# One batch in four of the attention probabilities: block transposes on VectorE and a round trip through DRAM in place of TensorE transposes

## The chip, the core and the metric

The program runs on one core of a Trainium2 chip. The metric is the device time of one execution in microseconds (us). The engines of the core are TensorE (PE in the profile; its weight loads are PEld), VectorE (DVE), ScalarE (ACT), GpSimd (POOL) and SyncE (SP). They work side by side and wait for each other by semaphores only; here SP issues all the transfers (DMAs), in one fixed order.

## What is computed

The inputs are `x` of 128 batches x 32 rows x 1024 columns and a context of 128 x 257 x 256, all float32. Three residual blocks follow each other:

```python
x = x + xattn(layernorm(x), ctx, ctx)   # 32 heads, 8 key groups, head size 32, softmax over 257 keys
x = x + s4(layernorm(x))                # a causal convolution of length 1024 along the columns, plus a skip
x = x + moe(layernorm(x))               # rank-8 experts: top 16 of 64, 512 bottleneck columns
```

The change concerns the first block alone. There, for each batch and each of the 8 key groups, the 4 heads of the group x 32 rows give 128 rows of scores over 256 keys (the 257th key is handled apart), and the probabilities of these 128 rows must be turned, keys onto partitions, before TensorE can multiply them with the values.

## The kernel before

Four batches x 32 rows make one tile of 128 rows, so there are 32 tiles. The work of a tile is spread over three iterations: iteration `it` does the attention of tile `it` up to its second batch, ends the attention of tile `it-1` (batches 2 and 3) and does its convolution, and does the experts of tile `it-2`. The head (tiles 0 and 1, with the preparation of the weights) and the tail (tile 31 and what is left) are written out one call after the other. The order of the calls on each engine is written out by hand and fixed; an engine that meets a wait stands still with all that is behind it in its order.

The attention of a tile, batch `b` of four:

- `scores(it, b)` (PE, 24 matmuls, L573) writes 8 groups x 256 scores into four PSUM banks that are held once, so it waits until the maxima of the batch before are done.
- `maximum(it, n)` (DVE, L1398), n = 8b + g, adds the mask, writes the negated scores to `ms` and their minimum to `negmax`. `exp(it, n)` (ACT, L851) writes the probabilities into `pr[:, b % 2, g, :]` and their sums into `den`.
- `pair_chunk(it, m)` (PE, L561) turns two groups of `pr`, four 128x128 transposes into one of four PSUM banks (`ps_p`); `pair_copy(it, m)` (ACT, L783) copies the bank, 128x512, to `pts`. m runs from 0 to 15, four for each batch.
- `attend(it, hh)` (PE, 32 matmuls for two calls, L593), hh = 2b and 2b + 1, multiplies `pts` with the context `cx`; `output(it, b)` (ACT) copies the result out.
- `move_den(it, b)` (SP, L381) moves the sums with four small transfers; `normalisers(it)` (DVE, L1454) needs them of all four batches. GpSimd then makes the share of the last key and the residual, and `out_half`, `u_stats`, `row_norm` and `u_chunk` lead into the convolution.

All other transposes (`out_chunk`, `u_chunk`, `z_chunk`, `gated_chunk`) use the same helper at L561. `convolve` is L632, `experts` L647, `expand` L660. `q_turn` (DVE, L1405) already turns the queries, 128x512, in 32x32 blocks, after a trip through DRAM (`store_q`, `move_q`). Which bank a product uses is looked up in the table `BANKS`, and a product waits for the reader of what the bank held before. The tables of banks and the orders are all that a call's place depends on.

Of the kernel before, what the change touches and what calls it, by code (L numbers as in the profile page):

```python
# [27 lines left out]
P = 128  # L28
BPT = P // SEQ
TILES = BATCHES // BPT  # L30
HALVES = 2
# [4 lines left out]
PAIRS = STEPS // 2  # L36
# [31 lines left out]
    "pair": (1, 0, 0, 1, 0, 2, 0, 3, 1, 0, 0, 1, 0, 3, 1, 0,),  # L68
    "out": (0, 1,),
    "u": (3, 1,),  # L70
    "z": (0, 3,),
    "g": (1,),
    "y": (2, 1,),
    "f": (3, 2,),
    "b": (1, 2,),
    "o": (3, 2, 1, 1,),
    "keys": (3,),
    "router": (3,),
    "sums": (1,),
    "dft": (0,),  # L80
    "rows": (1,),
    "strip": (2, 3, 2,),
    "w": (0, 2, 0, 1, 2, 3, 2, 2, 3, 2, 1, 2, 3, 0, 1, 3,),
# [17 lines left out]
def at(tile, per, k):  # L101

    return tile * per + k

# [7 lines left out]
def build(nc, io):  # L112
    ctx = ExitStack()
    with ctx:
# [65 lines left out]
        turn_q = nc.dram_tensor("turn_q", [BPT, SEQ, DIM], F32, kind="Internal").ap()  # L180
        turn = nc.dram_tensor("turn", [BPT, SEQ, HEADS], F32, kind="Internal").ap()
# [23 lines left out]
        e_done = sem("e_done")  # L205
        pt_done = sem("pt_done")
# [108 lines left out]
        def _(sp):  # L315
# [126 lines left out]
            def iteration(it, odd):  # L442
                if on(it - 1):
                    load_context(it - 1, 2)
                turn_last(it)
                if on(it - 1):
                    load_residual(it - 1)
                if on(it - 3):
                    store(it - 3)
                if on(it - 1):  # L450
                    move_den(it - 1, 2)
                    move_den(it - 1, 3)
                if on(it + 1):
                    load_keys(it + 1, 0)
                load_context(it, 0)
                load_context(it, 3)
                load_context(it, 1)
                if on(it + 1):
                    load_last(it + 1)
                    load_keys(it + 1, 1)  # L460
                    store_q(it + 1)
                    load_keys(it + 1, 2)
                    move_q(it + 1)
                move_den(it, 1)
                move_den(it, 0)
                if on(it + 2):
                    load_x(it + 2)
                if on(it + 1):
                    load_keys(it + 1, 3)
                    store_last(it + 1)  # L470
            load_s4(); load_x(0); load_router(); load_wide(); load_context(0, 2); load_mask(); load_keys(0, 0)
            load_last(0); load_weight(0); load_keys(0, 1); store_q(0); clear_kernel(); load_weight(1); load_weight(2)
            move_q(0); load_x(1); load_keys(0, 2); load_weight(3); store_last(0); load_context(0, 0); turn_last(0)
            load_keys(0, 3); load_context(0, 3); load_last(1); load_keys(1, 0); store_q(1); load_weight(4)
            load_keys(1, 1); move_q(1); load_x(2); load_context(0, 1); move_den(0, 0); load_weight(5); load_keys(1, 2)
            load_weight(6); load_weight(7); store_last(1); load_keys(1, 3); turn_last(1); store_kernel()
            move_den(0, 1); load_strip(); move_den(0, 2); load_residual(0); move_den(0, 3); load_keys(2, 0)
            load_context(1, 0); load_context(1, 1); load_keys(2, 1); load_keys(2, 2); load_last(2); store_q(2)
            load_context(1, 3); move_den(1, 0); move_q(2); load_keys(2, 3); load_x(3); move_den(1, 1); store_last(2)
            for it in range(HEAD, TAIL):  # L480
                iteration(it, odd=it % 2)
            load_residual(30); load_context(31, 0); store(28); turn_last(31); load_context(30, 2); move_den(30, 2)
# [1225 lines left out]
```

## Time and profile before

| | |
|---|---|
| median of 3 runs | 1290.93 us (1287.35 to 1291.11) |
| the profiled execution | 1286.13 us, of which 1284.3 us are the span from the first to the last instruction |
| busy share of the span | PE 96%, ACT 87%, DVE 76%, POOL 64% |
| granted TensorE clock | 0.993 of full speed in the mean, 1.00 after the first stretch |
| DMA | 166.38 MB, mean 130 GB/s |
| one iteration in the steady part | 37.73 us |

The page of a profile gives the busy time of each engine, the chain of work that ended last (followed back from the last instruction, at each step to what released it), the costliest groups of instructions and the transfers. Further views group instructions by line and shape, list the waits, or show the instructions of a stretch in order of time. A matmul's duration includes its way through the array, and matmuls overlap, so the cost of a matmul is read from the distance between starts or from the chain, not from its mean duration.

### The profile page before, as it was taken

The page shows a single profiled execution, that of the slowest core. Times are in us where ns is not written, and L with a number is a line of the kernel's source. Part 1 is how long each engine was busy: PE and PEld are TensorE (multiplying, and loading weights), DVE is VectorE, ACT ScalarE, POOL GpSimd, SP SyncE. Part 2 cuts the span into 40 slices and gives each one's busy share as a digit, 9 for nine tenths or more (in the row PEclk, how much of TensorE's full clock was granted, in tenths as well). Part 3 has the DMA queues.
Part 4 walks back from the last instruction along what each step waited for, and adds up shares of the span by engine and source line. Part 5 has one row for each costly group of instructions (what it writes and reads, how often), then busy time and mean ns, then how long its engine had stood idle before and what let it go on. Part 6 is the DMA issues. An engine that isn't in the chain of part 4 may idle for free.

```text
span 1284.3 us, 41514 instructions
## 1 busy us (share of the span) xinstructions
PE 1238.2 (96%) x13676; PEld 1075.3 (84%) x13676; DVE 976.1 (76%) x3424; ACT 1121.2 (87%) x3337; POOL 827.1 (64%) x1259
## 2 busy tenths in 40 slices
PE   4679999999999999999999999999999999999997
PEld 3568888888888888888888888888888888888886
DVE  7877777877777777777877877778777777777753
ACT  6999999999899989898998989999998999899851
POOL 5477667677666667766767766676776666677420
PEclk9799999999999999999999999999999999999999
DMA  7543444444443444444344444444444434444210
GB/s 246 158 148 114 139 120 137 139 130 139 130 139 109 148 138 123 130 146 125 117 139 155 122 122 147 117 133 139 137 138 123 139 118 139 138 124 127 55 60 33
DMA packets 150103, 166.38 MB, mean 130 GB/s; under 512 B 58217, under 2 KB 116082, under 8 KB 149890
## 3 DMA queue, kind: packets, MB, share of 16 engines
q1 hardware_dynamic: 149890, 163.72, 42.7%
q8 instruction: 112, 1.84, 0.6%
q14 instruction: 101, 0.83, 0.2%
HBM read 128.50 MB, written 34.08 MB: 127 GB/s over the span
## 4 chain that ended last, share of the span: by engine, by line
PE 93%; ACT 2%; DVE 2%; DMA 1%; issue 1%; POOL 0%; SPq 0%; DVEq 0%; ACTq 0%; POOLq 0%
PE ps_p L561 27%; PE ps_p L647 17%; PE ps_p L632 17%; PE ps_p L660 14%; PE ps_p L593 10%; PE ps_s L573 9%; ACT pr L851 1%; DMA tmp<-in_wide 0%; ACT pts L783 0%; DMA qx<-turn_q 0%; DVE ms L1398 0%; DVE x L1254 0%; PE ps_p L519 0%; DMA turn_q<-xq 0%; ACT xq L865 0%
## 5 line engine op out<-in xcount | busy, mean ns | idle before, releaser
L851 ACT ACTIVATE pr<-ms,negmax 128x256 f32<-128x256 f32 x1024 | 513.8, 505 | 1.4 <-DVE negmax L1398 1.3
L1398 DVE CUSTOM_DVE_ANT_0 ms<-ps_s,neg_mask,last 128x256 f32<-128x256 f32 x1024 | 455.2, 473 | 55.4 <-PE ps_s L573 55.1
L783 ACT ACTIVATE pts<-ps_p 128x512 f32<-128x512 f32 x512 | 296.4, 593 | 51.4 <-PE ps_p L561 47.5
L561 PE MATMUL ps_p<-ident,pr 128*128 128x128 f32 x2048 | 305.2, 277 | 9.6 <-ACT pr L851 3.5
L561 PEld LDWEIGHTS ps_p<-ident,pr 128*128 128x128 f32 x2048 | 239.2, 141 | 46.1 <-issue 13.7
L851 ACT ACTIVATION_READ_ACCUMULATOR pr<-ms,negmax 128x1 f32 x1024 | 200.4, 196 | 0.0
L1072 POOL TENSOR_TENSOR kt<-kr,kt 128x512 fp32r<-128x512 f32 x128 | 165.6, 1293 | 29.5 <-ACT kt L783 29.5
L647 PE MATMUL ps_p<-wa_hi,ut_hi 128*128 128x288 f32 x512 | 177.6, 347 | 1.4 <-DVE ut_lo L1214 1.4
L647 PE MATMUL ps_p<-wa_lo,ut_hi 128*128 128x288 f32 x512 | 151.2, 295 | 0.0
L647 PE MATMUL ps_p<-wa_hi,ut_lo 128*128 128x288 f32 x512 | 150.6, 294 | 0.0
L1114 POOL TENSOR_TENSOR lastp<-lastp 128x256 f32<-128x256 f32 (+4 forms) x320 | 129.8, 405 | 22.6
L593 PE MATMUL ps_p<-pts,cx 128*32 128x128 f32 x4096 | 138.4, 276 | 3.5 <-DVE wb_lo L1226 2.6
L632 PE MATMUL ps_p<-strip_hi,ut_hi 128*128 128x512 f32 (+2 forms) x384 | 138.2, 360 | 0.4 <-DVE tmp L1482 0.4
L1095 POOL TENSOR_TENSOR qs<-qr,qs 128x512 fp32r<-128x512 f32 x64 | 82.9, 1295 | 80.7 <-ACT qs L783 80.7
L632 PE MATMUL ps_p<-strip_hi,ut_lo 128*128 128x512 f32 (+2 forms) x384 | 133.4, 347 | 0.0
L632 PE MATMUL ps_p<-strip_lo,ut_hi 128*128 128x512 f32 (+2 forms) x384 | 133.4, 347 | 0.0
L573 PE MATMUL ps_s<-kt,qs 32*128 32x256 f32 x3072 | 128.0, 298 | 0.0
L783 ACT ACTIVATE ut_hi<-ps_p 128x512 fp32r<-128x512 f32 x128 | 76.2, 596 | 57.3 <-PE ps_p L561 57.3
L593 PEld LDWEIGHTS ps_p<-pts,cx 128*32 128x32 f32 x4096 | 104.1, 109 | 24.7 <-issue 18.3
L573 PEld LDWEIGHTS ps_s<-kt,qs 32*128 32x128 f32 x3072 | 101.6, 187 | 21.9 <-issue 21.8
L660 PE MATMUL ps_p<-wb_hi,zt_hi 128*128 128x512 f32 x256 | 110.9, 433 | 3.0 <-DVE zt_lo L1214 3.0
L1152 POOL TENSOR_TENSOR x<-x,tmp 128x512 f32<-128x512 f32 x64 | 81.0, 1291 | 45.7 <-DVE x L1464 45.7
(139 smaller groups left out, 2562.5 us busy)
## 6 DMA issues: line engine op xcount, KB each, us to landing
cx<-in_ctx SPq DMA_DIRECT2D x128, 256.0 KB, 3.1
kr<-in_keys SPq DMA_DIRECT2D x128, 256.0 KB, 3.7
xq<-in_x SPq DMA_DIRECT2D x32, 512.0 KB, 4.0
turn_q<-xq SPq DMA_DIRECT2D x32, 512.0 KB, 3.7
qx<-turn_q SPq DMA_DIRECT2D x128, 128.0 KB, 2.9
xr<-in_x SPq DMA_DIRECT2D x32, 512.0 KB, 4.3
out_x<-tmp SPq DMA_DIRECT2D x32, 512.0 KB, 5.1
dn<-den SPq DMA_DIRECT2D x512, 2.0 KB, 1.8
```

Source lines behind the costliest of these rows:

```text
L561: mm = pe.transpose(into[:, j * P:(j + 1) * P], source, ident[:, :])
L573: mm = pe.matmul(ps_s[:, quad, h * SW:(h + 1) * SW], qs[rs, it % 2, q_part, b, h, :, :].rearrange("p r s -> p (r s)"), kt[rs, b, k_part, h ...
L593: mm = pe.matmul(product("o", b, it)[HEAD_DIM * q:HEAD_DIM * (q + 1), h * P:(h + 1) * P], cx[:, b, j, g * HEAD_DIM:(g + 1) * HEAD_DIM], pt ...
L632: mm = pe.matmul(product("y", k, tile)[:, o0:512], u[:, c, :], s[:, s0:s0 + w], start=(c == 0 and j == 0), stop=(c == 4 * k + 3 and j == 2 ...
L647: mm = pe.matmul(product("f", k, tile)[:, 0:ZB], u[:, c, :], w[:, c, k * ZB:(k + 1) * ZB], start=(c == 0 and j == 0), stop=(c == FC - 1 an ...
L660: mm = pe.matmul(product("b", k, tile)[:, :], u[:, c, :], w[:, c, k * 512:(k + 1) * 512], start=(c == 0 and j == 0), stop=(c == BC - 1 and ...
L783: return act.activation(out, in_, ACT.Copy, scale=scale)
L851: act.activation(pr[:, b % 2, g, :], ms[:, n % MS, :], ACT.Exp, bias=negmax[:, n % MS:n % MS + 1], scale=-1.0, accum_out=den[:, b, g:g + 1 ...
L1072: pool.tensor_tensor(kt[:, b, 1, :, :], kr[:, at(tile, BPT, b) % KRS, :, :], kt[:, b, 0, :, :].bitcast(F32), ALU.subtract).then_inc(kl_don ...
L1095: pool.tensor_tensor(qs[:, tile % 2, 1, :, h, :, :], qr[:, :, :, :], qs[:, tile % 2, 0, :, h, :, :].bitcast(F32), ALU.subtract).then_inc(q ...
L1114: pool.tensor_tensor(near, near, far, ALU.add).then_inc(ls_done, 1)
L1398: dve.tensor_tensor_reduce(ms[:, n % MS, :], ps_s[:, g % GPH, g // GPH * SW:(g // GPH + 1) * SW], neg_mask[:, 0:SW], 1.0, last[:, it % 2, ...
```

## The change

For batch 2 of each tile (`TURNED = (2,)`) the four `pair_chunk` and the four `pair_copy` are gone. Instead:

1. `exp` of that batch writes its 256 probabilities in runs of 32 to strided places, so that each half of `pr` (four groups, 1024 columns) is laid out in 32x32 blocks by key block.
2. `p_turn(it, 0, h)` (DVE), for the halves h = 0 and 1, transposes 128x1024 in place, block by block.
3. `store_p(it, 0, h)` (SP) writes the half, 512 KB, to the DRAM tensor `turn_p`; `load_p(it, 0)` waits for both stores, and reads the whole back with four transfers of 256 KB, each onto 32 partitions of `pts`.
4. `attend(it, 4)` and `attend(it, 5)` wait for the load, and read `pts` through a strided view as their moving operand.

The table of banks and the orders on all engines are new. What matters of the order on SP: `load_p(it-1, 0)` stands before `move_den` of batches 2 and 3, and `store_p(it-1, 0, 0)` stands behind the store of the output, which waits for `third_residual`. `exp` now waits for the reader of its own half of `pr` (two batches back) and not for all of the batch before.

```diff
-PAIRS = STEPS // 2
+TURNED = (2,)
...
+            def store_p(it, k, h):
+                sp.wait_ge(p_turned[k][h], at(it, 1, 1))
+                if at(it, 64, 0) > 0:
+                    sp.wait_ge(p_loaded[k], at(it, 64, 0))
+                sp.dma_start(turn_p[k, :, :, h, :],
+                             pr[:, TURNED[k] % 2, GPH * h:GPH * (h + 1), :]).then_inc(p_stored[k][h], 16)
+
+            def load_p(it, k):
+                b = TURNED[k]
+                for h in range(HALVES):
+                    sp.wait_ge(p_stored[k][h], at(it, 16, 16))
+                if at(it, 2 * BPT, 2 * b - 2) > 0:
+                    sp.wait_ge(pv_done, at(it, 2 * BPT, 2 * b - 2))
+                own = pts[:, b % 2 * GPH:(b % 2 + 1) * GPH, :]
+                for i in range(GPH):
+                    sp.dma_start(own[SEQ * i:SEQ * (i + 1), :, :],
+                                 turn_p[k, :, i, :, :].rearrange("(r t) h c -> t r (h c)", r=REP)).then_inc(p_loaded[k], 16)
...
             def attend(it, hh):
                 b, h = hh // 2, hh % 2
-                pe.wait_ge(pc_done, at(it, PAIRS, 2 * hh + 2))
+                if b in TURNED:
+                    pe.wait_ge(p_loaded[TURNED.index(b)], at(it, 64, 64))
+                else:
+                    pe.wait_ge(pc_done, at(it, PAIRS, paired(2 * hh + 2)))
+                turned = pts[:, b % 2 * GPH:(b % 2 + 1) * GPH, :].rearrange("p r (h j q s) -> p h j q r s", h=HALVES, j=TBLK, q=GPH)
...
+                                       turned[:, h, j, q, :, :] if b in TURNED else
                                        pts[:, (2 * hh + q // 2) % PTS, (2 * (q % 2) + j) * P:(2 * (q % 2) + j + 1) * P],
...
-                act.activation(pr[:, b % 2, g, :], ms[:, n % MS, :], ACT.Exp,
+                out, masked = pr[:, b % 2, g, :], ms[:, n % MS, :]
+                if b in TURNED:
+                    out = pr[:, b % 2, g // GPH * GPH:(g // GPH + 1) * GPH, :].rearrange("p g c -> p (g c)").rearrange(
+                        "p (i j g t) -> p g j i t", i=GPH, j=TBLK, g=GPH)[:, g % GPH, :, :, :]
+                    masked = masked.rearrange("p (j i t) -> p j i t", j=TBLK, i=GPH)
+                act.activation(out, masked, ACT.Exp,
...
+            def p_turn(it, k, h):
+                b = TURNED[k]
+                dve.wait_ge(e_done, at(it, STEPS, GROUPS * b + GPH * (h + 1)))
+                half = pr[:, b % 2, GPH * h:GPH * (h + 1), :].rearrange("p g c -> p (g c)")
+                dve.transpose(half, half).then_inc(p_turned[k][h], 1)
```

The new orders, cut to the calls that the prediction speaks of. On PE, iteration `it` (steady part): `pair_chunk(it-1, 12)`; `scores(it, 0)`; `pair_chunk(it-1, 13)`, `14`; `experts(it-2, 1)` whole, 24 matmuls; `pair_chunk(it-1, 15)`; `pair_chunk(it, 0)`; `attend(it-1, 4)`, `5`; `pair_chunk(it, 1)`; `scores(it, 1)`; `attend(it-1, 6)`, `7`; `pair_chunk(it, 2)`, `3`, both `out_chunk` and `experts(it-2, 0)` in three parts; `scores(it, 2)`; `pair_chunk(it, 4)`; `gated_chunk`; `attend(it, 0)`, `1`; `pair_chunk(it, 5)`, `6`; `expand` 18 matmuls; `scores(it, 3)`; `pair_chunk(it, 7)`; both `u_chunk`; `expand` 6 matmuls; `convolve` whole; `z_chunk`; `attend(it, 2)`, `3`; `z_chunk`.

On DVE: ..., `maximum(it, 23)`, `third_residual(it-2, 0)`, `p_turn(it, 0, 0)`, `maximum(it, 24)`, `q_turn`, `u_low(0)`, `maximum(it, 25)`, `26`, `u_low(1)`, `maximum(it, 27)`, `p_turn(it, 0, 1)`, `third_residual(it-2, 1)`, `maximum(it, 28)`, ... On ACT: ..., `exp(it, 20)`, `row_norm`, `pair_copy(it, 6)`, `u_high(0)`, `exp(it, 21)`, `u_high(1)`, `k_high(it+1, 1)`, `exp(it, 22)`, `exp(it, 23)`, ... On SP: `store(it-3)`, `store_p(it-1, 0, 0)`, `store_p(it-1, 0, 1)`, `load_residual(it-1)`, `load_context(it-1, 2)`, `turn_last(it)`, `load_p(it-1, 0)`, `move_den(it-1, 2)`, `move_den(it-1, 3)`, ...

## Rows read from the trace of the kernel before

**Rows 1.** The page's busy us, share of the span and instructions, by engine.

```profile
PE 1238.2 (96%) x13676; PEld 1075.3 (84%) x13676; DVE 976.1 (76%) x3424; ACT 1121.2 (87%) x3337; POOL 827.1 (64%) x1259
```

**Rows 2.** The page's chain that ended last, by engine and by line.

```profile
PE 93%; ACT 2%; DVE 2%; DMA 1%; issue 1%; POOL 0%; SPq 0%; DVEq 0%; ACTq 0%; POOLq 0%
PE ps_p L561 27%; PE ps_p L647 17%; PE ps_p L632 17%; PE ps_p L660 14%; PE ps_p L593 10%; PE ps_s L573 9%; ACT pr L851 1%; DMA tmp<-in_wide 0%; ACT pts L783 0%; DMA qx<-turn_q 0%; DVE ms L1398 0%; DVE x L1254 0%; PE ps_p L519 0%; DMA turn_q<-xq 0%; ACT xq L865 0%
```

**Rows 3.** One steady period: busy us by engine, clock, DMA share, GB/s.

```profile
586.00:623.73 37.73, 37.73 (x425) 32.90 (x425) 28.83 (x105) 34.27 (x105) 25.75 (x40) 1.00 0.45 138
```

**Rows 4.** The chain, start us and us: the same piece 26 periods apart.

```profile
171.00 4.00 PE ps_p L632 x21
...
1151.89 4.00 PE ps_p L632 x21
```

**Rows 5.** Pieces of the chain within one period: start us, us, what.

```profile
590.43 1.01 PE ps_p L593 x32
...
592.03 0.91 PE ps_s L573 x20
...
594.36 0.44 PE ps_p L561 x4
594.79 0.80 PE ps_p L647 x6
...
611.26 0.58 PE ps_p L561 x4
611.85 2.77 PE ps_p L660 x12
```

**Rows 6.** Groups by line and shape: the exponentials, the removed copies, the block transpose.

```profile
L851 ACT ACTIVATE pr<-ms,negmax 128x256 f32<-128x256 f32 x1024 | 513.8, 505 | 1.4 <-DVE negmax L1398 1.3
...
L783 ACT ACTIVATE pts<-ps_p 128x512 f32<-128x512 f32 x512 | 296.4, 593 | 51.4 <-PE ps_p L561 47.5
...
L1405 DVE STREAM_TRANSPOSE qr<-qx 128x512 f32<-128x512 f32 x64 | 44.9, 702 | 1.7 <-DMA qx<-turn_q 1.2 <-issue 0.3
```

**Rows 7.** Instructions in order of time, ACT and DVE: start us, us.

```profile
586.91 0.59 ACT L783 ACTIVATE pts<-ps_p 128x512 f32<-128x512 f32 x1
587.39 0.51 ACT L851 ACTIVATE pr<-ms,negmax 128x256 f32<-128x256 f32 x1
...
586.51 0.69 DVE L1405 STREAM_TRANSPOSE qr<-qx 128x512 f32<-128x512 f32 x1
587.13 0.44 DVE L1398 CUSTOM_DVE_ANT_0 ms<-ps_s,neg_mask,last 128x256 f32<-128x256 f32 x1
```

**Rows 8.** SP's issues in order of time: start us, us, number of transfers.

```profile
589.40 0.34 SPq L436 DMA_DIRECT2D xr<-in_x  x1
589.80 0.42 SPq L440 DMA_DIRECT2D out_x<-tmp  x1
591.71 5.92 SPq L381 DMA_DIRECT2D dn<-den  x8
...
611.71 2.21 SPq L402 DMA_DIRECT2D qx<-turn_q  x4
```

**Rows 9.** Transfers, KB and us to landing (589.4 to 595.2, then all); one microsecond's rate.

```profile
xr<-in_x SPq DMA_DIRECT2D x1, 512.0 KB, 4.3
out_x<-tmp SPq DMA_DIRECT2D x1, 512.0 KB, 5.2
...
cx<-in_ctx SPq DMA_DIRECT2D x128, 256.0 KB, 3.1
...
593.00:594.00 1.00, 1.00 (x10) 1.00 (x11) 1.00 (x4) 0.87 (x4) 0.00 (x0) 1.00 1.02 414
```

**Rows 10.** Landing times of the output's stores, then of the context's loads.

```profile
DMA to landing us min/median/max: 2.6/5.1/7.3
...
DMA to landing us min/median/max: 2.6/3.1/6.7
```

**Rows 11.** Waits over the whole span: us in total, times, longest us.

```profile
DVE dn L1454 <- DMA dn<-den: 33.6, 29, 2.0
```

More of the change, by code:

```diff
@@ L103, in at, with paired @@
     return tile * per + k
+def paired(m):
+    return sum(k // GPH not in TURNED for k in range(m))
+PAIRS = paired(STEPS // 2)
 def wait(eng, sem, value):
@@ L446, in iteration @@
                 if on(it - 1):
[L447 to L450, printed above, removed]
+                    load_p(it - 1, 0)
                     move_den(it - 1, 2)
@@ L472, in _ @@
[L472 to L476, printed above, removed]
@@ L485, in _ @@
+            store(30); store(31)
             sp.wait_ge(out_stored, 16 * TILES)
@@ L755, in _ @@
[L755 to L758 removed]
+            weight_chunk(0, 0); keys_transpose(); weight_chunk(0, 1); router_product(); weight_chunk(1, 0)
@@ L759, in _ @@
+            u_chunk(0, 1); pair_chunk(1, 7); convolve(0, 0, 0, 4); convolve(0, 1, 0, 2); convolve(0, 1, 2, 8)
+            z_chunk(0, 0, 0); attend(1, 3); z_chunk(0, 1, 0)
             for it in range(HEAD, TAIL):
                 iteration(it, odd=it % 2)
-            pair_chunk(30, 11); pair_chunk(30, 12); scores(31, 0); experts(29, 1, 0, 1); pair_chunk(30, 13)
-            pair_chunk(30, 14); experts(29, 1, 1, 2); pair_chunk(30, 15); experts(29, 1, 2, 5); attend(30, 4)
-            attend(30, 5); experts(29, 1, 5, 8); pair_chunk(31, 0); scores(31, 1); experts(29, 0, 0, 2)
@@ L764, in _ @@
-            pair_chunk(31, 1); attend(30, 6); attend(30, 7); experts(29, 0, 2, 3); pair_chunk(31, 2)
-            pair_chunk(31, 3); experts(29, 0, 3, 5); out_chunk(30, 0); experts(29, 0, 5, 6); out_chunk(30, 1)
-            experts(29, 0, 6, 8); pair_chunk(31, 4); scores(31, 2); gated_chunk(29); pair_chunk(31, 5); attend(31, 0)
-            attend(31, 1); pair_chunk(31, 6); expand(29, 0, 0, 3); pair_chunk(31, 7); expand(29, 0, 3, 4)
-            expand(29, 1, 0, 3); pair_chunk(31, 8); u_chunk(30, 0); expand(29, 1, 3, 4); u_chunk(30, 1)
@@ L769, in _ @@
[L769 to L773 removed]
+            scores(31, 0); pair_chunk(30, 12); pair_chunk(30, 13); pair_chunk(30, 14); experts(29, 1, 0, 1)
@@ new lines, in _ @@
+            pair_chunk(31, 6); expand(29, 0, 0, 3); expand(29, 0, 3, 4); expand(29, 1, 0, 3); pair_chunk(31, 7)
+            u_chunk(30, 0); expand(29, 1, 3, 4); scores(31, 3); u_chunk(30, 1); convolve(30, 0, 0, 4)
+            convolve(30, 1, 0, 1); convolve(30, 1, 1, 8); z_chunk(30, 0, 0); attend(31, 2); z_chunk(30, 1, 0)
+            pair_chunk(31, 12); attend(31, 3); pair_chunk(31, 13); pair_chunk(31, 14); experts(30, 1, 0, 2)
+            experts(30, 1, 2, 4); experts(30, 1, 4, 8); pair_chunk(31, 15); attend(31, 4); attend(31, 5)
```

527 lines of the change are left out of this document (264 added, 263 removed).

## The prediction

> **What bounds the kernel now.** I read the page's busy shares first: PE is busy for 96% of the span, ACT for 87%, DVE for 76% [rows 1]. A busy share alone doesn't say what sets the end, so the chain of waits came next: 93% of it is PE, and 27 of 100 parts of the span are the transposes of L561 alone, more than any other line [rows 2]. Then one period of the steady part: PE is busy for all of its 37.73 us, at full granted clock, while DVE has 8.9 us free, ACT 3.5 and the 16 DMA engines 55% [rows 3]. The same piece of the chain returns after 26 periods at a distance of 980.89 us, 37.73 each [rows 4]: no period differs from the next. So PE is the bound for the 29 iterations of the loop, some 1094 us, and time taken from PE is time taken from the kernel, as long as nothing it waits for comes later than now.
>
> **What a turned batch gives back on PE.** In the chain a `pair_chunk` between other matmuls costs 0.44 us, though the mean duration of its four transposes would suggest more; one that follows `attend` costs 0.58 us [rows 5]. The extra 0.14 goes with the change of shape and not with the chunk: the number of places where something follows `scores` or `attend` stays about the same in the new order. I take 0.44. Four chunks a tile, 32 tiles: 128 x 0.44 = 56.3 us. A period would be 37.73 - 1.76 = 35.97 us. The moving around of `experts`, `expand` and `convolve` changes no instruction; I cost it at nothing, and keep 0.2 us a period to both sides for it.
>
> **ACT.** Four copies a tile go; from the start of one to the start of what follows is 0.48 us [rows 7], so 1.92 us a period. ACT is then busy for 34.27 - 1.92 = 32.35 of 35.97 us, 90%. Nothing on the path, since ACT isn't on it now. The eight `exp` of batch 2 write in runs of 32 to strided places. No row shows such a write. Below nothing is excluded, as it is the same 256 elements; above I bound it by the copy's cost for 512 elements against the exp's for 256, 0.59 to 0.51 us [rows 6, 7], 0.1 us each, 0.8 a period, and PE's cover holds both. I take nothing.
>
> **DVE.** Two block transposes of 128x1024 a tile. The one of 128x512 lasts 0.70 us in the mean and the next instruction starts 0.62 us after it [rows 6, 7]. Twice the columns: at most 2 x 0.62 = 1.24 us, and not less than 0.62; I take 1.2, so 2.4 a period, and DVE is busy for 31.2 of 35.97 us, 87%. That it still fits is not that it is free: the second one stands ahead of `third_residual(it-2, 1)`, on which the output's store waits, and ahead of `maximum(it, 28)` to `31`, on which the next `scores` wait. Its cover is the time in which PE does `convolve`, 36 matmuls, of which 21 take 4.0 us [rows 4]; DVE has four maxima, two residuals and two splits there. With the cover gone it would cost its 1.2 us each period, 35 us in all.
>
> **DMA.** 1 MB out and 1 MB back a tile, 67 MB more on 166. The engines' share goes from 0.45 to about 0.45 x 233/166 x 37.73/35.97 = 0.66. They have carried 414 GB/s in one microsecond [rows 9], so the bytes fit. The latency is what counts, and so does SP, a single queue: six more issues a tile, about 0.42 to 0.55 us each [rows 8], 3 us of a period.
>
> **The new path.** What is late if something is late: `attend(it-1, 4)` now waits for the load, and behind it stand all of PE's calls. I follow the path from the end of `exp(it-1, 23)`:
>
> - `p_turn(.., 1)`: 1.2 us (above).
> - `third_residual`, before which SP doesn't get past the output's store: 0.6 us, as a DVE instruction of 512 columns [rows 7].
> - SP issues the output's store and `store_p` of half 0: 0.9 us until the second half's issue begins.
> - Landing of that one. Of two transfers of 512 KB issued 0.4 us apart the first landed after 4.3 us and the second after 5.2 [rows 8, 9]. A third adds another 0.9: 6.1 us.
> - `load_p`: four issues of 0.44 to 0.55 us; the last begins 1.3 to 1.7 us after the first, and a 256 KB load lands in 3.1 us [rows 8, 9]. 1 MB at 414 GB/s needs 2.5 us, so the rate doesn't add much. 5.0 us.
>
> Sum 13.8 us. This closes a loop, since `exp(it, 23)` can't come before PE has done what lies between `attend(it-1, 4)` and the second `u_chunk` of the same iteration (ACT reads it in `u_high(1)`, ahead of exps 22 and 23). That is, by rows 5: three pairs of `attend` 3.0, three `scores` 2.7, twelve chunks of transposes 5.3, 24 matmuls of `experts` at 0.133 = 3.2, 18 of `expand` at 0.231 = 4.2, six changes of shape 0.9: 19.3 us. Behind it on ACT two copies and two exps, 2.0 us, and 0.2 to hand over: 21.5 us. The loop is 21.5 + 13.8 = 35.3 us long against PE's 35.97. It closes, with 0.7 us to spare. Landing times scatter from 2.6 to 7.3 us [rows 10], so now and then it won't. The same queue feeds a second loop: `move_den` of batches 2 and 3 stands behind `load_p`. DVE already waits for these sums in 29 tiles, 1.2 us in the mean [rows 11], and they will come later by the four issues, 2.2 us, plus what SP waits ahead of `load_p`. The maxima of batch 1, for which `scores(it, 2)` waits, now stand behind `normalisers`. For both together I charge 0.25 us a period, 7.5 us in all.
>
> **Head and tail** hold 8 of the 128 chunks, counted above. PE isn't always the bound there, so up to 3 us of their share may not come; the new order may give as much. Nothing taken.
>
> **The sum.** 1286.1 (the profiled execution) - 56.3 + 7.5 = 1237.3 us. The median of the runs is 1290.93, 0.37% above the profiled execution; 1237.3 x 1.0037 = 1242 us is the forecast. What a measurement of this kernel can tell from no change is about 0.3%, 4 us.
>
> **Rivals.**
>
> 1. *The turned path is a little longer than the loop allows, and takes part of the gain.* The path has room for 35.97 - 21.5 = 14.5 us. At 15.4 us the period is 36.9, the gain 0.83 us a period, and the time 1290.9 - 0.83 x 32 = 1264 us. For it: three stores at once were never seen in this kernel, and the second was already 0.9 us later than the first. Against: the room of 0.7 us.
>
> 2. *No change: each load goes at half rate.* The four loads land on 32 partitions each. If such a load runs at half of 414 GB/s, 1 MB takes 5.1 us and not 2.5, the path is 13.8 + 2.5 = 16.3, the period 37.8 us, and all that PE gave back is spent in front of `attend(it-1, 4)`: 1293 us. Against: the queries' loads, also four onto 32 partitions, go out in 2.21 us [rows 8] and DVE hardly waits for them, 1.2 us in the whole span [rows 6]. The Trainium skill has this rule ("SBUF — State Buffer", section "Door 1: The DMA port swizzle"): partitions 0 to 31, and 0 to 63 too, are reached through 8 of 16 ports, at about half the rate. By the page alone, the time would be this rival's; no row here shows a large load onto 32 partitions, so it keeps a chance of its own.
>
> 3. *Slower: `attend(it-1, 4)` waits, every iteration, longer than the four chunks lasted.* One mechanism: the chain turn, store, load in front of PE. It decides from a path of 37.73 - 21.5 = 16.2 us on. At 17 us the period is 38.5, +0.8 us in 29 periods, about 1314 us; with the slowest landings of rows 10 in place of mine (7.3 for 6.1, 6.7 for 3.1) the path is 18.6 and the period 40.1, about 1360 us. For it: 67 MB more on the same engines, behind one queue. Against: those landings are the extremes of 32 and 128.
>
> 4. *The strided reads of `attend` are slow.* Its moving operand is now four runs of 32. No row shows one. If it streams at half rate, the two calls cost 1.0 us more [rows 5] a period: 1274 us. The other end is nothing. I take nothing, as the exps and copies with reshaped views cost what plain ones do. The page named above (section "Door 1") says that a read stays at full rate with two or more hits in each line of 16 bytes, which runs of 32 have; by it, this rival is nothing.
>
> **Chances.** The forecast, with the loop closed up to 0.5 us a period, 0.53; it spans 1230 to 1255. Rival 1 0.22 (1255 to 1285), rival 4 0.05, rival 2 0.08, rival 3 0.12. Faster 0.80, same 0.07, slower 0.13. The range goes from 1228, all of the 56.3 us and a little from the order, to 1283, which leaves out rivals 2 and 3: together 0.20.
>
> **What would show it.** In the changed kernel's profile: the distance between two returns of the same piece of `convolve` in the chain, 36.0 to 36.5 us (a), and PE busy for all of a period (b). L561 over `pr` down to 1536 transposes, the copies to 384. The block transposes at 1.2 to 1.3 us, 64 of them (c). Landing of the two `turn_p` stores at 5 to 6 us, and of the loads at 3 to 4 us (d): 5 us or more means rival 2. `attend`'s matmuls at a pace of 1.01 us for 32, also in batch 2 (e). If PE shows waits for the DMA of `pts`, the path is too long: rival 1 with up to 1.7 us a period, rival 3 above. If `maximum` waits for `dn`, it is the second loop. What makes the prediction wrong most easily is that I summed the path from single transfers, while here three stores, a residual's load and a context's load are in flight together, and nobody but SP can start the next.

## The result, and the profile after

The changed kernel takes 1349.95 us in the median of four runs (1345.48 to 1353.5), against 1289.77 us for the kernel before (1287.35 to 1291.11): 1.046 of its time, 95% interval 1.043 to 1.050. It is slower by 60 us, where 1242 us were forecast.

The page of the kernel after, busy us by engine and then the chain by engine and line, answers to [rows 1, 2]:

```profile
PE 1205.8 (90%) x13164; PEld 1040.5 (77%) x13164; DVE 1041.9 (78%) x3488; ACT 1062.4 (79%) x3209; POOL 822.2 (61%) x1259
...
PE 57%; DMA 16%; issue 9%; SPq 7%; DVE 7%; ACT 3%; POOL 1%; DVEq 0%; ACTq 0%; POOLq 0%
PE ps_p L598 14%; PE ps_p L702 11%; DMA pts<-turn_p 10%; PE ps_p L674 8%; PE ps_p L689 8%; PE ps_p L634 8%; PE ps_s L610 7%; DMA turn_p<-pr 5%; DVE ms L1427 3%; SPq L458 2%; SPq L411 2%; ACT pr L884 1%; DMA last<-turn 1%; SPq L400 1%; DVE t
```

The transposes (L598 now, 14% of the chain for 27%) did shrink, but PE is no longer alone on the path: transfers, SP and VectorE hold some 30% of it. The span grew from 1284.3 to 1343.7 us. By the first matmul of each tile's convolution, 5.9 us of that lie ahead of tile 0's, 47.6 us between the first and the thirtieth after it (39.3 us a period, from 38.0 to 41.8, for 37.7), and 5.9 us behind.

The waits of the whole span, us in total, times, longest us, say where PE's idle time comes from:

```profile
DVE ms L1427 <- issue: 110.4, 30, 6.0
ACT pr L884 <- DVE negmax L1427: 111.6, 35, 5.9
PE ps_p L598 <- ACT pr L884: 55.4, 30, 4.1
PEld ps_p L634 <- DMA pts<-turn_p: 35.0, 31, 5.0
PE ps_p L634 <- DMA pts<-turn_p: 27.7, 29, 4.8
```

There are two. `attend(it-1, 4)` waits for the loads of the turned probabilities, as the prediction feared, but this is the smaller one, 27.7 us of PE's time. The larger one is 3.7 us in each of 30 tiles ahead of `maximum(it, 0)`. "issue" means that the profile shows no releaser. Scores are there; what that instruction needs besides is `last`, which `turn_last(it)` brings with four transfers of 4 KB (the second run below bears this out). Then `exp` waits for the maximum, and PE for the `exp`, 55.4 us in all. Both waits lie ahead of the same `attend(it-1, 4)`, since `pair_chunk(it, 0)` stands in front of it. In one tile (in square brackets the idle time just before, and what ended it):

```profile
623.85 0.48 DVE L1427 CUSTOM_DVE_ANT_0 ms<-ps_s,neg_mask,last 128x256 f32<-128x256 f32 x1 [3.87 <-issue]
...
626.00 0.66 PE L598 MATMUL ps_p<-ident,pr 128*128 128x128 f32 x4 [1.97 <-ACT pr L884]
626.94 1.91 PE L634 MATMUL ps_p<-pts,cx 128*32 128x128 f32 x32 [0.28 <-DMA pts<-turn_p]
```

The chain over the path of the same tile, start us, us, what:

```profile
610.73 0.03 DVE pr L1435
...
611.87 0.66 DVE tmp L1517
612.55 0.34 SPq L470
...
612.99 0.58 SPq L400
...
613.67 6.08 DMA turn_p<-pr
...
619.80 0.30 SPq L411
...
621.09 5.80 DMA pts<-turn_p
626.94 1.91 PE ps_p L634 x32
```

From the start of the block transpose (610.70) to `attend` it is 16.24 us (16.3 in the median of the loop's tiles), where the prediction summed 13.8 and set the limit at 16.2. The store's landing, 6.08 us, is what was forecast. The load's part is not: 7.14 us from the first issue to `attend`, for 5.0.

SP in the same stretch (start us, us, number of transfers), then the stretch in steps of 2 us (busy us of PE, PEld, DVE, ACT, POOL; clock; DMA share; GB/s):

```profile
612.55 0.34 SPq L470 DMA_DIRECT2D out_x<-tmp  x1
612.99 1.32 SPq L400 DMA_DIRECT2D turn_p<-pr  x2
614.35 1.29 SPq L466 DMA_DIRECT2D xr<-in_x  x1
615.69 1.25 SPq L374 DMA_DIRECT2D cx<-in_ctx  x1
617.06 2.50 SPq L458 DMA_DIRECT2D last<-turn  x4
619.80 2.26 SPq L411 DMA_DIRECT2D pts<-turn_p  x4
```

```profile
614.00:616.00 2.00, 2.00 (x15) 1.88 (x14) 1.92 (x6) 1.77 (x6) 0.33 (x2) 1.00 1.01 379
616.00:618.00 2.00, 2.00 (x42) 1.64 (x41) 1.60 (x3) 1.08 (x3) 2.00 (x3) 1.00 1.03 311
...
620.00:622.00 2.00, 2.00 (x18) 2.00 (x17) 0.00 (x0) 0.61 (x2) 0.00 (x0) 1.00 1.04 273
622.00:624.00 2.00, 2.00 (x16) 1.79 (x15) 0.15 (x1) 0.00 (x0) 0.00 (x0) 1.00 0.97 238
624.00:626.00 2.00, 0.03 (x1) 0.00 (x1) 1.97 (x9) 1.63 (x6) 0.00 (x0) 1.00 0.86 173
626.00:628.00 2.00, 1.72 (x27) 1.47 (x31) 1.73 (x10) 2.00 (x7) 1.73 (x3) 0.75 0.09 11
628.00:630.00 2.00, 2.00 (x24) 1.28 (x18) 1.90 (x11) 1.46 (x6) 1.07 (x4) 0.50 0.66 212
630.00:632.00 2.00, 2.00 (x56) 1.67 (x56) 1.00 (x4) 2.00 (x8) 1.83 (x5) 0.89 0.86 263
```

Between 612.55 and 616.9 SP hands out 2.25 MB; the 16 KB of `turn_last` come behind them, at 617.06, which is 4.5 us after the output's store. The kernel before issued them at 587.29, 2.5 us ahead of its output's store (589.80 in [rows 8]). They land in 4.2 us in the median, for 1.7 before. All 16 DMA engines are busy from 614 to 624, and yet the rate falls from 379 to 238 GB/s as the loads come in. The issue of one transfer takes 1.25 to 1.29 us here, for 0.34 to 0.42 in [rows 8]. PE stands still from 624 to 626. Its granted clock is still 1.00 when it starts again, and 0.50, its lower level, from 627.0 to 630.4: the two calls of `attend` cost 1.91 us for the 1.01 of [rows 5].

### The profile page after: what moved, and what is told of

The parts are those of the page before. It is cut to its first block, busy times and chain, and to the rows that moved or that the text cites. A ratio compares the mean times of both kernels' runs of the same rounds, so it can differ in the third digit from the quotient of the medians.

```text
span 1343.7 us, 40582 instructions
## 1 busy us (share of the span) xinstructions
PE 1205.8 (90%) x13164; PEld 1040.5 (77%) x13164; DVE 1041.9 (78%) x3488; ACT 1062.4 (79%) x3209; POOL 822.2 (61%) x1259
## 3 DMA queue, kind: packets, MB, share of 16 engines
q8 instruction: 107, 1.75, 0.5%
## 4 chain that ended last, share of the span: by engine, by line
PE 57%; DMA 16%; issue 9%; SPq 7%; DVE 7%; ACT 3%; POOL 1%; DVEq 0%; ACTq 0%; POOLq 0%
PE ps_p L598 14%; PE ps_p L702 11%; DMA pts<-turn_p 10%; PE ps_p L674 8%; PE ps_p L689 8%; PE ps_p L634 8%; PE ps_s L610 7%; DMA turn_p<-pr 5%; DVE ms L1427 3%; SPq L458 2%; SPq L411 2%; ACT pr L884 1%; DMA last<-turn 1%; SPq L400 1%; DVE tmp L1517 1%
## 5 line engine op out<-in xcount | busy, mean ns | idle before, releaser
L1427 DVE CUSTOM_DVE_ANT_0 ms<-ps_s,neg_mask,last 128x256 f32<-128x256 f32 x1024 | 452.1, 477 | 158.9 <-issue 110.4
L598 PE MATMUL ps_p<-ident,pr 128*128 128x128 f32 x1536 | 241.3, 288 | 59.1 <-ACT pr L884 55.4
L598 PEld LDWEIGHTS ps_p<-ident,pr 128*128 128x128 f32 x1536 | 174.7, 145 | 102.5 <-ACT pr L884 69.0
L809 ACT ACTIVATE pts<-ps_p 128x512 f32<-128x512 f32 x384 | 222.1, 587 | 33.2 <-PE ps_p L598 16.7
L1108 POOL TENSOR_SCALAR lns<-lns 128x1 f32<-128x1 f32 x96 | 18.3, 191 | 281.2 <-DVE lns L1466 280.0
L634 PE MATMUL ps_p<-pts,cx 128*32 128x128 f32 x4096 | 151.1, 291 | 29.0 <-DMA pts<-turn_p 27.7
L689 PE MATMUL ps_p<-wa_hi,ut_hi 128*128 128x288 f32 x512 | 162.3, 317 | 1.4 <-DVE ut_lo L1243 1.4
L634 PEld LDWEIGHTS ps_p<-pts,cx 128*32 128x32 f32 x4096 | 111.6, 115 | 54.0 <-DMA pts<-turn_p 35.0
L610 PE MATMUL ps_s<-kt,qs 32*128 32x256 f32 x3072 | 133.5, 306 | 10.7 <-DVE negmax L1427 9.9
L610 PEld LDWEIGHTS ps_s<-kt,qs 32*128 32x128 f32 x3072 | 107.3, 197 | 41.0 <-issue 41.0
L1243 DVE TENSOR_TENSOR ut_lo<-ps_p,ut_hi 128x512 fp32r<-128x512 f32 x128 | 88.3, 690 | 36.8 <-ACT ut_hi L809 36.5
```

The costliest lines, as they stand in the source:

```text
L598: mm = pe.transpose(into[:, j * P:(j + 1) * P], source, ident[:, :])
L610: mm = pe.matmul(ps_s[:, quad, h * SW:(h + 1) * SW], qs[rs, it % 2, q_part, b, h, :, :].rearrange("p r s -> p (r s)"), kt[rs, b, k_part, h ...
L634: mm = pe.matmul(product("o", b, it)[HEAD_DIM * q:HEAD_DIM * (q + 1), h * P:(h + 1) * P], cx[:, b, j, g * HEAD_DIM:(g + 1) * HEAD_DIM], tu ...
L689: mm = pe.matmul(product("f", k, tile)[:, 0:ZB], u[:, c, :], w[:, c, k * ZB:(k + 1) * ZB], start=(c == 0 and j == 0), stop=(c == FC - 1 an ...
L809: return act.activation(out, in_, ACT.Copy, scale=scale)
L1243: return dve.tensor_tensor(lo, source, hi.bitcast(F32), ALU.subtract).then_inc(done, 1)
```

## The experiments

Each was compared with the kernel before in the same session, whose median lay between 1288.5 and 1291.9 us. Ratios with their 95% intervals:

| the changed kernel with | us | ratio to before |
|---|---|---|
| nothing else | 1350 | 1.046 (1.043 to 1.050) |
| other data loaded, no wait for the stores | 1342 | 1.040 (1.036 to 1.044) |
| small loads right behind the stores | 1416 | 1.098 (1.094 to 1.103) |
| loads onto 128 partitions, other arrangement | 1311 | 1.016 (1.012 to 1.019) |
| small loads ahead, residual and context elsewhere | 1342 | 1.042 (1.036 to 1.047) |
| loads by row block, 128 partitions | 1591 | 1.233 (1.231 to 1.234) |
| small loads first | 1429 | 1.107 (1.105 to 1.109) |
| loads by row block and small loads first | 1648 | 1.276 (1.273 to 1.280) |
| ... and first half's store early | 1614 | 1.249 (1.247 to 1.251) |
| **A**: loads onto 128 partitions, keys interleaved | 1310 | 1.016 (1.012 to 1.019) |
| A and small loads first | 1372 | 1.063 (1.060 to 1.065) |
| ... and first half's store early | 1344 | 1.040 (1.036 to 1.044) |
| ... and context early, residual late | 1367 | 1.060 (1.056 to 1.063) |
| **B**: first half's store early, alone | 1296 | 1.004 (1.001 to 1.007) |
| A and B | 1258 | 0.975 (0.972 to 0.979) |
| order by readiness, without A, with B | 1314 | 1.016 (1.012 to 1.020) |
| order by readiness, with A, without B | 1296 | 1.003 (1.000 to 1.006) |
| **order by readiness, A and B** | 1247 | 0.965 (0.962 to 0.969) |

**Round trip, order, or partitions?** The first four set three causes against each other. In the first the loads read context rows in place of the turned probabilities:

```diff
-                for h in range(HALVES):
-                    sp.wait_ge(p_stored[k][h], at(it, 16, 16))
...
-                                 turn_p[k, :, i, :, :].rearrange("(r t) h c -> t r (h c)", r=REP)).then_inc(p_loaded[k], 16)
+                                 context[it * BPT + i, 0:2 * P, :].rearrange("(r t c) f -> t r (c f)", r=REP, t=SEQ)).then_inc(p_loaded[k], 16)
```

> The changed kernel, but load_p reads the same 1 MB, in pieces of the same size, from the context in DRAM and doesn't wait for the two stores (so the probabilities of batch 2 are not the ones multiplied). Theory A, the round trip (the store must land before the load may start): the path in front of attend(it-1, 4) loses the wait, the period falls from 38.9 us to 36.5 or less, the time to about 1275. Theory B, SP and the burst (SP comes to load_p only when the stores have landed anyway, behind 2.75 MB of transfers and four small ones that it could issue only slowly): the period stays at 38.5 to 39, the time within 0.7% of 1350.

1342 us. Loads that don't wait for the stores gain next to nothing: in the changed kernel SP, when it comes to `load_p`, waits for the stores in 10 of 32 tiles only, 4.8 us in all. So the order in which the round trip has to go isn't what costs.

```diff
                     store_p(it - 1, 0, 1)
+                turn_last(it)
...
                     load_residual(it - 1)
                     load_context(it - 1, 2)
-                turn_last(it)
...
                     load_p(it - 1, 0)
```

> The changed kernel with turn_last issued right behind the two stores of probabilities, ahead of the residual's load and the context's. Theory B: last<-turn lands some 3 us earlier, maximum(it, 0) no longer waits 4 us for it, and the wait for exp in front of pair_chunk goes. But load_p still lands as late as before, so the period falls by 1 us at most: 1320 to 1345. Theory A says the same for the load and gives the maxima no part in it: 1345 to 1350. If the late maxima alone were the cause, the period would fall by 2 us or more: 1290 or less.

1416 us, a miss. The wait ahead of the maximum all but goes (13.1 us in all), but the residual and the context, 0.75 MB, now stand directly ahead of the slow loads, which land in 6.5 us for 5.1: PE waits 136.4 us for them, and VectorE 138.0 us for `dn`, whose moves stand behind them.

```diff
-                    sp.dma_start(own[SEQ * i:SEQ * (i + 1), :, :],
-                                 turn_p[k, :, i, :, :].rearrange("(r t) h c -> t r (h c)", r=REP)).then_inc(p_loaded[k], 16)
+                    sp.dma_start(own[:, i, :],
+                                 turn_p[k, :, i, :, :].rearrange("p h c -> p (h c)")).then_inc(p_loaded[k], 16)
```

> The changed kernel with the load of the turned batch as four transfers of 256 KB onto all 128 partitions each, in place of four onto 32 (same bytes, same pieces of 2 KB, another arrangement, so batch 2 is multiplied with wrongly placed probabilities). Theory C, a load onto 32 partitions is slow: the loads land in 3 to 4 us and not in 5 to 6, the path is 2 us shorter, the period 37 to 37.5, the time 1290 to 1305. Theory B without C: the engines' total rate was the limit, landing and time as in the changed kernel within 0.7%.

1311 us: 39 us for the wider loads, with the same bytes and issues. A load lands in 3.8 us for 5.1, and PE waits 6.4 us for them, for 27.7. The wait ahead of the maximum stays, 95.4 us.

```diff
-                    load_residual(it - 1)
-                    load_context(it - 1, 2)
+                    if it == HEAD:
+                        load_context(it - 1, 2)
                 turn_last(it)
...
                     load_p(it - 1, 0)
                     move_den(it - 1, 2)
                     move_den(it - 1, 3)
+                    load_residual(it - 1)
...
+                load_context(it, 2)
                 move_den(it, 0)
```

> The changed kernel with SP's order changed alone: turn_last right behind the stores, load_p behind it, the residual's load behind move_den, and the context's load of batch 2 half an iteration earlier. Theory B: both waits shrink, load_p lands 2 to 3 us earlier (0.75 MB less in front of it) and the maxima start with scores(it, 0); period 36.5 to 37.3, time 1265 to 1295. Theory A: the round trip is as long as before, period 38.5 to 39. Theory C: a gain of 1 us at most.

1342 us, a miss again. More than half of the wait ahead of the maximum goes (46.7 us left), and PE's wait for the loads, 76.0 us for 27.7, takes its place. This order doesn't mend it while the loads are slow.

**Loads onto 128 partitions with the data in place.** The first cut is by row block:

```diff
+                for r in range(REP):
+                    sp.dma_start(own[:, r, :],
+                                 turn_p[k, SEQ * r:SEQ * (r + 1), :, :, :].rearrange("t i h c -> i t (h c)")).then_inc(p_loaded[k], 16)
```

> Only the four loads of the turned probabilities are cut another way: each fills all 128 partitions with 2 KB pieces (one of the four row blocks of the tile for all four groups) in place of 32 partitions with 8 KB each; the same bytes, the same number of pieces and issues, and the right data. Theory C (a load onto 32 partitions fills slowly, whatever it reads): as the other load onto 128 partitions, 1305 to 1316 us, landing near 3.8 us, and no wait of TensorE's attend for them. Rival (the gain of that run came from the order in which it read DRAM, piece after piece of the same tensor row): 1325 to 1350, landing near 5.

1591 us. The stretch while little else was in flight, columns as above:

```profile
634.00:636.00 2.00, 1.18 (x10) 0.94 (x8) 0.86 (x5) 0.34 (x1) 0.00 (x0) 1.00 0.27 99
636.00:638.00 2.00, 0.66 (x4) 0.42 (x4) 1.97 (x9) 2.00 (x8) 0.53 (x2) 1.00 0.29 105
638.00:640.00 2.00, 0.00 (x0) 0.00 (x0) 1.73 (x10) 1.71 (x6) 1.50 (x2) 1.00 0.29 98
```

The share of busy DMA engines is 0.27 to 0.29 at some 100 GB/s: about 4 of 16. The outermost dimension on the DRAM side has 4 elements here, and 32 or 128 in all other forms. The Trainium skill says just this ("DMA: Bandwidth & Descriptors", section "Why a DMA increments its semaphore by 16 and not by 1"): the number of engines is the largest up to 16 that divides the outermost dimension of both sides. The share in these rows agrees.

The small loads were put first in three runs: once with the loads onto 32 partitions, and twice with those on 4 engines, alone and with the first half's store early.

```diff
+                turn_last(it)
                 if on(it - 3):
                     store(it - 3)
...
-                turn_last(it)
```

> Only the order of SP is changed: the four small loads of the last logits stand first in an iteration, ahead of the output's store, so that they meet an empty queue; the loads of the turned probabilities stay on 32 partitions. Theory T (two costs that add: the small loads late behind the burst, and the slow loads onto 32 partitions): VectorE's wait of 3.7 us a period at the first maximum goes, but each store is issued 1.8 us later and the big loads are again directly in front of the slow ones, so attend waits longer: 1345 to 1400. Rival R (the late small loads are the whole of what is left of the loss): 1290 to 1320.

1429 us, more than either theory had said. VectorE no longer waits at the maximum, but PE waits 142.5 us for the loads.

> Both edits: loads on 128 partitions, and the four small loads first. Theory T: both waits of TensorE in the path's window are gone, 1245 to 1280 us, a period of 36.0 to 37.0. Rival R2 (what is left is the bytes themselves: 3 MB in 12 us, so that taking one transfer forward sets another back): 1300 or more, and VectorE or TensorE waits for another transfer of the burst.

> Both edits, and the first half's store (512 KB) issued at the end of the iteration before, about 6 us earlier than the second half's, so that 0.5 MB leave the burst. Theory T: no slower than the run before it, 1240 to 1270 us. Rival R2 (the bytes in the burst): clearly faster than the run before it, by 1% or more, since a sixth of the burst is gone.

1648 and 1614 us: with loads on 4 engines neither says anything about theory T.

The second cut lets partition 4t+i hold key 64i+32j+t, so that both sides have 128 in the outermost place; the context rows of batch 2 come in the same order (edit **A**):

```diff
-                    masked = masked.rearrange("p (j i t) -> p j i t", j=TBLK, i=GPH)
+                    masked = masked.rearrange("p (i j t) -> p j i t", j=TBLK, i=GPH)
...
+                for r in range(REP):
+                    sp.dma_start(own[:, r, :],
+                                 turn_p[k, SEQ * r:SEQ * (r + 1), :, :, :].rearrange("t i h c -> (t i) (h c)")).then_inc(p_loaded[k], 16)
...
+                             rows_in.rearrange("o (i j t) f -> (o t) (i j) f", j=TBLK, i=GPH) if b in TURNED else
```

> The four loads of the turned probabilities go onto 128 partitions with the right data, and the access pattern's outermost dimension is 128 on both sides (partition 4t+i holds key 64i+32j+t, the context rows of that batch are loaded in the same order; no other bytes, pieces or issues). Theory D (in the run of 1591 us the loads were slow because their outermost dimension on the DRAM side was 4, so that only 4 of the 16 DMA engines carried them): 1305 to 1320 us, landing near 3.8 us. Rival (a correct split into rows is slow in itself, by where it reads in DRAM): 1450 or more.

1310 us, landing 3.7 us. So the 1591 us came from the outermost dimension, and the 39 us of the earlier run don't hang on its other arrangement. One thing these runs don't take apart: from 32 to 128 partitions the outermost dimension of the load goes from 32 to 128 too.

**What holds the other 20 us and the gain?** Three more orders on top of A. The first is `turn_last(it)` ahead of `store(it-3)`, the diff of the run of 1429 us:

> The same loads, and the four small loads of the last logits first in an iteration of SP. Theory T (the late small loads are what is left): VectorE's wait at the first maximum goes, 1245 to 1285 us. Rival R2 (the bytes of the burst): 1300 or more, since the stores and all behind them are issued 1.8 us later, and TensorE waits for the turned probabilities again.

```diff
-                    store_p(it - 1, 0, 0)
...
                     load_keys(it + 1, 3)
+                store_p(it, 0, 0)
```

> As the run before, and the first half's store (512 KB) at the end of the iteration before. Theory T: 1240 to 1280 us, within 1% of the run before it. Rival R2: faster than the run before it by more than 1%.

```diff
                     store_p(it - 1, 0, 1)
-                    load_residual(it - 1)
-                    load_context(it - 1, 2)
...
                     load_p(it - 1, 0)
+                    load_residual(it - 1)
...
+                load_context(it, 2)
...
                     store_last(it + 1)
```

> As the run before, and the context rows loaded at the end of the iteration before, the residual behind the turned probabilities, so that only the output and one store (1 MB) stand ahead of the loads. Rival R2 (what queues ahead in bytes sets the landing): the fastest of the four, 1235 to 1260 us, with the period near 36.0. Theory T alone: within 0.5% of the run before it; or slower where the later residual makes GpSimd wait.

1372, 1344 and 1367 us. Theory T, that the late small loads only have to come first, falls. Rival R2, the bytes, is right in the first two and falls in the third, for which it had 1235 to 1260 us. In this third run, VectorE's block transpose and SP's issues (start us, us), then pieces of the chain:

```profile
623.34 1.24 DVE L1440 STREAM_TRANSPOSE pr<-pr 128x1024 f32<-128x1024 f32 x1
...
624.80 0.55 SPq L451 DMA_DIRECT2D turn<-lasts  x1
...
627.24 2.13 SPq L460 DMA_DIRECT2D last<-turn  x4
629.41 0.43 SPq L472 DMA_DIRECT2D out_x<-tmp  x1
630.28 0.54 SPq L402 DMA_DIRECT2D turn_p<-pr  x1
```

```profile
624.80 2.43 DMA turn<-lasts
...
630.28 4.10 DMA turn_p<-pr
...
635.75 5.27 DMA pts<-turn_p
...
641.06 1.93 PE ps_p L639 x32
```

The second half is turned at 624.6, but its store is issued at 630.28: SP first waits 2.4 us for the store that `turn_last` reads back, and then issues its four loads. From the start of the block transpose to `attend` it is now 17.7 us, more than the 16.24 of the changed kernel, though the loads are quick. And `move_den`, behind the loads, is late too: VectorE waits 156.4 us for `dn`. So SP is to do each thing when it becomes ready. This is the head of its iteration as it stands in the next run, on top of edit A, with the early store of the first half (edit **B**, the last line; lines left out are marked):

```python
                    store_p(it - 1, 0, 1)
                turn_last(it)
                if on(it - 3):
                    store(it - 3)
                if on(it - 1):
                    load_context(it - 1, 2)
                    load_p(it - 1, 0)
                    load_residual(it - 1)
                    move_den(it - 1, 2)
                    move_den(it - 1, 3)
...
                move_den(it, 1)
                store_p(it, 0, 0)
```

> Loads on 128 partitions through all 16 DMA engines, and SP's order by readiness: the first half's store right after the moves of the second batch's denominators, the second half's store first in the iteration (1 us after its block transpose), then the four small loads, the output's store, the context, the loads of the turned probabilities, the residual, the other denominators. Theory S (what is left is the place in SP's queue): from the last block transpose to attend 10 to 12 us, no wait of TensorE for the turned probabilities and less than 1 us a period at the first maximum: 1240 to 1265 us. Rival (the added bytes as such): 1290 or more.

1247 us: 3.5% faster than the kernel before. One period of it, columns as in [rows 3]; SP's issues; pieces of the chain:

```profile
607.28:642.79 35.51, 35.51 (x410) 31.16 (x409) 31.06 (x107) 32.35 (x100) 26.00 (x41) 1.00 0.65 200
```

```profile
604.06 0.59 SPq L402 DMA_DIRECT2D turn_p<-pr  x1
...
610.21 0.58 SPq L402 DMA_DIRECT2D turn_p<-pr  x1
610.91 2.54 SPq L460 DMA_DIRECT2D last<-turn  x4
613.50 0.43 SPq L472 DMA_DIRECT2D out_x<-tmp  x1
613.98 0.69 SPq L375 DMA_DIRECT2D cx<-in_ctx  x1
614.78 2.05 SPq L413 DMA_DIRECT2D pts<-turn_p  x4
```

```profile
607.28 6.61 PE ps_p L678 x36
...
614.33 1.01 PE ps_p L638 x32
...
618.30 3.21 PE ps_p L693 x24
621.51 0.87 PE ps_p L602 x8
622.38 1.01 PE ps_p L638 x32
...
642.79 6.61 PE ps_p L678 x36
```

From one `convolve` to the next it is 35.51 us, and PE is busy all through them, at full clock. The block transpose ends at 609.84, the store goes out 0.4 us later, and `attend(it-1, 4)` starts at 622.38 without a wait. Ten of the 30 periods last 35.5 to 35.6 us. In others PE still stops: it waits 10.8 us in 12 tiles for the loads, and VectorE 52.7 us for `dn`. So the time is that of theory S, but not all of its signs.

The remaining four take the three parts (A, B, the order) apart. The order and B, without A:

> The same order of SP with the loads as the change has them, onto 32 partitions. If the slow loads cost the 2 to 3 us of the path that they cost in the order of the change, and the path has slack of 2 to 3 us in this order: 1255 to 1300 us. Rival (the 32 partitions cost by holding up everything behind them in the queue, whatever the slack): 1300 to 1350.

1314 us: not in the range of the path's slack but of the rival. Both are seen in it: PE waits 70.1 us for the loads, for 10.8, and VectorE 106.4 us for `dn`, for 52.7.

The order and A, without B:

```diff
-                    if it == HEAD:
-                        store_p(it - 1, 0, 0)
+                    store_p(it - 1, 0, 0)
                     store_p(it - 1, 0, 1)
                 turn_last(it)
...
-                store_p(it, 0, 0)
```

> As the first of these three, but the first half's store directly ahead of the second's, as in the change. The two stores then move 1 MB where the path runs, so that the landing takes 1.2 us or so more, and the four small loads stand behind it: no slower than 1% against the first of these three, 1245 to 1275 us. Rival (the bytes decide): 1290 or more.

1296 us, a miss: the second 0.5 MB in front cost 3.9% here. In one tile the four small issues take 3.41 us for 2.54, and the loads 5.58 us from the last issue; PE waits 40.8 us for them, for 10.8.

A and B in the change's own order, and then B alone:

```diff
-                    store_p(it - 1, 0, 0)
+                    if it == HEAD:
+                        store_p(it - 1, 0, 0)
                     store_p(it - 1, 0, 1)
                     load_residual(it - 1)
...
                 move_den(it, 1)
+                store_p(it, 0, 0)
```

> Loads on 128 partitions through all 16 DMA engines, the first half's store right after the moves of the second batch's denominators, and else the order of the change: output, second half's store, residual, context, four small loads, turned probabilities. If the bytes ahead of the small loads decide (1.75 MB in place of 2.25 MB): the wait at the first maximum shrinks from 3.2 to 1 to 2 us a period, 1255 to 1285 us. If the order by readiness is what counts: 1290 to 1310 us, as without the earlier store.

1258 us: with the loads mended, taking one 512 KB store out of the burst is worth 52 us, and the rest of the order 11. The wait ahead of the maximum falls from 97.0 to 48.6 us.

> The change with one edit: the first half's store right after the moves of the second batch's denominators; the loads stay on 32 partitions, else the order of the change. If the two causes add (the late store costs 52 us beside the mended loads, the loads 39 us beside the late store): 1290 to 1305 us. If the slow loads also cost by what they hold up in the queue: 1305 to 1330. If the path has room now for the slow loads: 1255 to 1285.

1296 us. With late and early store the loads cost 1350 - 1310 = 40 and 1296 - 1258 = 38 us; with slow and quick loads the late store costs 54 and 52 us. In the change's own order the two add.

## Why the prediction was wrong

- *What a turned batch gives back on PE*: the term of the chunks is right, the one of the order is not. Where nothing waits, in the run of 1247 us, a period is 35.51 us, for 35.97 forecast: 2.2 us less than before, and not 1.76. By the chain, the transposes have 26.3% of 35.51 us for 29.4% of 37.73, which is 1.75 us less. Most of the other 0.47 us is `experts` (17.9% for 18.0%, 0.4 us less): the same 48 matmuls, in fewer and longer runs. The moving around was costed at nothing. Over 30 periods the mean is 36.2, as the forecast has it with its 0.25 us charged, but this is luck: the order gives more, and PE stops for longer. L598 stands over 1536 transposes, and the copies are 384. `attend`'s strided reads cost 1.01 us for 32, also in batch 2: rival 4 didn't happen.
- *ACT*: the `exp` has a mean of 501 ns for 505, the strided write shows no cost. *DVE*: 64 block transposes at 1.23 to 1.25 us, for 1.2. Its busy time in that period is 31.06 of 35.51 us, 87% as forecast.
- *Head and tail*: taken at nothing, with 3 us less from their chunks at most. The head took 5.9 us more, and 6.2 us in the run of 1247 us too. In it PE once waits 13.9 us for ScalarE's `x` (13.6 us in that run), where the longest wait before was 7.7 us; why wasn't looked into.
- *The new path*: summed at 13.8, measured at 16.24 us. Turn and residual 1.85 for 1.8, SP 1.1 for 0.9, landing of the third store 6.1 for 6.1. **The step that failed first is the load's leg**, "four issues ... and a 256 KB load lands in 3.1 us": 7.14 for 5.0. The 3.1 us came from loads onto 128 partitions; these fill 32. This was rival 2, held at 0.08; what spoke against it were the queries' transfers of 128 KB, which land in 2.9 us in both kernels and don't show how a large load goes. The rule of the Trainium skill that the prediction set beside that rival ("SBUF — State Buffer", section "Door 1: The DMA port swizzle") agrees with the landings of 5.1 and 3.7 us in direction; it speaks of about half the rate, and in this mixed stream the landing grew by 1.4 us. It is worth 38 to 40 us. By the prediction's own terms a path of 16.24 us makes a period of 37.7 us and the 1293 us of rival 2, not 1350: what is missing is in the next point. The other part of the loop, from `attend` to the next block transpose of a second half, was summed at 21.5. In the median it took 21.9 us in the run of 1247 us, beside a path of 13.7, and 22.6 us in the changed kernel, beside a path of 16.3.
- *The larger failure is a move that was not priced at all*, a wait taken at nothing without a reason: `turn_last(it)` now stands behind the output, both stores, the residual and the context. The prediction asked what `move_den` would wait for, found a second loop there, charged 0.25 us (it wasn't needed: VectorE waits 7.8 us for `dn` over the span, for 33.6 before), and forgot the other small transfer on the same queue, though its place was in the new order. VectorE's wait is 110.4 us over the span, and PE's for the `exp` behind it 55.4. Of the 2.25 MB ahead of it 1 MB is the two stores side by side; the first could have gone 6 us earlier, which is worth 52 to 54 us.
- *"The bytes fit"*: in the mean they do (share 0.65 at 35.51 us a period, 0.66 forecast). In the 10 us around the path they don't: all engines are busy, and each byte put in front delays what is behind.
- *The clock*: not thought of. The changed kernel and the run of 1247 us have the same 13164 PE instructions, busy for 1205.8 and 1179.8 us: by this, 26 of the 97 us between their spans are PE at its lower clock, and the other 71 are idle time. The mean granted clocks, 0.973 of 1343.7 us and 0.99 of 1246.5 us, lose 36 and 12 us, which agrees. That split is worked out from the two pages, not tested by a run.
- Rival 3 had the sign, and near 1360 us almost the number, but its mechanism, `attend` waiting for the path with landings of 7.3 and 6.7 us, is the lesser part of it (27.7 us of waits on PE): luck.

The sum of causes, mended in this order: 1350 - 1247 = 103 us, of which 40 are the loads' partitions, 52 the late first store, 11 the rest of SP's order. The last one holds only with the quick loads: with them it is worth 14 us with the late store too (1296 for 1310), while with slow loads the same order costs 18 us (1314 for 1296). Why is not settled; in that run PE waits 70.1 us for the loads, for 27.4 in the change's order, and VectorE 106.4 us for `dn`, behind them, for 9.0.

## What to carry to other kernels

When a transfer is added to a queue, list every transfer behind it, the smallest too, and ask for each who waits for it: 4 KB behind 2.25 MB landed in 4.2 us here, for 1.7. Start a store when its data are ready and not where its partner is; a burst's length matters more than the mean share of the DMA engines. Price a load by a row of the same size, the same number of partitions and the same outermost dimension, and where no row is of that kind, don't let a row of another size speak against a known rule.

## What the hardware showed beside this

- The same 1 MB in four loads, in the same order of transfers: 5.1 us to land onto 32 partitions (outermost dimension 32), 3.7 onto 128 (outermost dimension 128); and at about 100 GB/s, a DMA share of 0.27 to 0.29, when the outermost dimension is 4.
- The issue of a transfer on SP takes 0.34 to 0.42 us in [rows 8], and 1.25 to 1.29 us for 512 and 256 KB with 1.5 to 2 MB handed out just before them. Four small loads of 4 KB take 1.75 us in the kernel before, 2.50 us in the changed one behind 2.25 MB, 2.54 us in the run of 1247 us behind 0.5 MB, and 3.41 us in that of 1296 us behind 1 MB: what was handed out just before doesn't set this alone.
- PE stood still for 2 us at 624, and 1 us after it had work again its granted clock fell to 0.50, from 627.0 to 630.4. A stop alone doesn't tell: from 663 to 667 in the same run PE was busy for 1.42 of 4 us, and its clock stayed at 1.00.
